# Spectral layers on one core: the last task's rows for the inverse W product loaded step by step into the first task's buffer, and held groups moved to other steps

## What is computed

```python
# layer 0
f = fft2(x, axes=(1, 2), norm='ortho'); Xh = (f.real - f.imag)[:, :, :46]
o1 = relu(einsum(Xk, w1[0]) + b1[0]); o2 = einsum(o1, w2[0]) + b2[0]
x = ifft2(softshrink(o2, 0.01), s=(H, W)).real + x
# layer 1
xf = rfft2(x, axes=(1, 2), norm='ortho')
o1r = relu(mm(xr, w1[0]) - mm(xi, w1[1]) + b1[0])
o1i = relu(mm(xi, w1[0]) + mm(xr, w1[1]) + b1[1])
o2r = softshrink(mm(o1r, w2[0]) - mm(o1i, w2[1]) + b2[0], 0.01)
o2i = softshrink(mm(o1i, w2[0]) + mm(o1r, w2[1]) + b2[1], 0.01)
y = irfft2(o2r + 1j * o2i, s=(H, W)) + x
```

## Time and profile before

| | |
|---|---|
| median of 3 runs | 519.47 us (517.39 to 521.99) |
| the profiled execution | 518.5 us |
| its span | 516.7 us |
| TensorE busy | 475.7 us, 92% |
| VectorE (DVE) / ScalarE (ACT) / GpSimd (POOL) busy | 59% / 41% / 34% |
| mean granted TensorE clock | 0.971 of full speed |
| DRAM read and written | 201 GB/s over the span |

### The profile page before, as it was taken

How to read it: one execution, slowest core, us unless ns; L and a number is a source line. 1 busy time by engine, 2 the same in 40 slices (tenths; PEclk the granted TensorE clock), 3 DMA queues, 4 the chain that set the end, 5 groups by cost and what they waited for, 6 DMA issues and landing times.

```text
span 516.7 us, 14864 instructions
## 1 busy us (share of the span) xinstructions
PE 475.7 (92%) x6144; PEld 341.0 (66%) x6144; DVE 306.7 (59%) x674; ACT 209.5 (41%) x473; POOL 173.1 (34%) x194
## 2 busy tenths in 40 slices
PE   3479999999999999999999999999999999998773
PEld 1157787767777677767777776767777777876531
DVE  6534455457754677457754677456764577567643
ACT  0025544643445443543354442554355433434201
POOL 9822313223341344223441244313442123222124
PEclk9859999999999999999999999999999999999967
DMA  8889763667989588977889688977989565644397
GB/s 182 264 229 258 198 192 91 148 204 193 261 230 238 158 229 245 231 207 186 256 238 219 173 198 256 234 201 182 261 222 256 158 176 158 145 100 129 114 257 226
DMA packets 76864, 104.63 MB, mean 203 GB/s; under 512 B 7777, under 2 KB 63319, under 8 KB 76798
## 3 DMA queue, kind: packets, MB, share of 16 engines
q1 hardware_dynamic: 57766, 56.74, 41.1%
q0 software_dynamic: 10608, 40.45, 29.5%
q10 hardware_dynamic: 8424, 6.49, 5.1%
HBM read 52.21 MB, written 51.43 MB: 201 GB/s over the span
## 4 chain that ended last, share of the span: by engine, by line
PE 79%; DVE 6%; DMA 6%; POOL 3%; ACT 2%; issue 2%; SPq 1%; ACTq 1%; POOLq 0%; DVEq 0%
PE ps L620 14%; PE ps L686 13%; PE ps L711 12%; PE ps L673 11%; PE ps L587 10%; PE ps L633 8%; PE ps L698 5%; PE ps L649 4%; PE ps L659 3%; DMA img<-x 2%; DVE img L566 2%; DVE ns L540 2%; POOL xs L384 2%; ACT p L457 1%; DVE nt L518 1%
## 5 line engine op out<-in xcount | busy, mean ns | idle before, releaser
L566 DVE TENSOR_TENSOR img<-ps,img 90x768 f32<-90x768 f32 x92 | 82.6, 900 | 20.3 <-PE ps L620 16.9
L384 POOL TENSOR_TENSOR xs<-xs,nt 128x360 f32<-128x360 f32 (+1 forms) x48 | 41.6, 866 | 147.9 <-DVE nt L518 120.6
L620 PE MATMUL ps<-jr,cst 64*90 64x384 f32 (+1 forms) x358 | 81.5, 525 | 6.7 <-DVE img L566 5.7
L587 PE MATMUL ps<-img,cst 128*64 128x384 f32 (+1 forms) x368 | 70.8, 500 | 9.7 <-DMA img<-x 9.7
L393 POOL DMA_DIRECT2D y<-img x42 | 34.8, 828 | 133.5 <-DVE img L566 133.2
L450 ACT ACTIVATE o<-ps,wt 97x180 f32<-97x180 f32 (+1 forms) x96 | 33.8, 406 | 107.6 <-PE ps L673 107.6
L633 PEld LDWEIGHTS ps<-cst,bt 128*64 128x64 f32 x1472 | 63.2, 141 | 20.4 <-issue 13.9
L540 DVE SCALAR_TENSOR_TENSOR ns<-p,ps 109x384 f32<-109x384 f32 x96 | 53.2, 554 | 37.8 <-ACT p L457 32.9
L633 PE MATMUL ps<-cst,bt 128*64 128x90 f32 x1472 | 69.0, 248 | 6.1 <-DMA bt<-scr_f 6.1
L686 PE MATMUL ps<-wt,o 128*64 128x96 f32 x1472 | 73.9, 249 | 0.2 <-DVE o L532 0.2
L686 PEld LDWEIGHTS ps<-wt,o 128*64 128x64 f32 x1472 | 64.9, 137 | 12.3 <-issue 12.3
(11 more groups left out here) (41 smaller groups left out, 403.0 us busy)
## 6 DMA issues: line engine op xcount, KB each, us to landing
y<-img POOLq DMA_DIRECT2D x35, 540.0 KB, 5.4
img<-x POOLq DMA_DIRECT2D x30, 540.0 KB, 8.3
scr_i<-et SPq DMA_DIRECT2D x48, 270.0 KB, 5.6
scr_f<-fs SPq DMA_DIRECT2D x154, 72.0 KB, 3.3
bt<-scr_f SPq DMA_DIRECT2D x40, 270.0 KB, 5.2
jr<-scr_i SPq DMA_DIRECT2D x48, 216.0 KB, 5.3
img<-x ACTq DMA_DIRECT2D x10, 540.0 KB, 6.9
y<-img SPq DMA_DIRECT2D x11, 270.0 KB, 3.5
```

The costliest lines, as they stand in the source:

```text
L384: nc.gpsimd.tensor_tensor(re, re, nt[s % 2][:, :, 0:kws(s), 0:H], ALU.subtract).then_inc(re_ok, 1)
L566: nc.vector.tensor_tensor(y, p, y, ALU.add).then_inc(i_add, 1)
L587: last = mm(ps[64 * r:64 * r + 64, P3 + g % 2, 0:(b - a) * HC], K["w_fwd"], img[t % IMGS][:, a:b, :].rearrange("p h c -> p (h c)"), start= ...
L620: last = mm(ps[0:W, B0 + r, 0:n], K["w_inv"][64 * r:64 * r + 64, :], set_rows(t, j)[64 * r:64 * r + 64, at, 0:n], start=True, stop=True)
```

## The change

- Held groups: loop steps 45, 46, 47 and 48 get 3, 3, 2 and 2 of them; groups 10 and 11 come behind the last inverse H product. `pair_of` gives these two the pairs P2 and P1.
- The last task's rows go into `f0`, all 12 groups. Behind the store of each step's inverse H product (from the second of task 7) SP waits for the store of the step before and loads that step's rows: 8 partitions of each half r for groups 0 to 10, and 8 for group 11, three transfers. The last step's rows are loaded at `last_rows`, half 0 and group 11 by SP, half 1 by ACT. The product of group 0 waits for all.
- The products of task 7 contract over 48 partitions (2 * KWP) instead of 64.
- LAST_POOL has three groups instead of four, with `p1` and one `et` buffer in turn. ACT issues the stores of these three, behind its last copy; SP the other nine.

```diff
--- before.py
+++ after.py
@@ -23,10 +23,11 @@
 STEPS = -(-KW // STEP)
 NSTEPS = TASKS * STEPS
 GROUPS = -(-H // 4)
+HELD = 10
 XCH = 8
 NXC = -(-H // XCH)
 IMGS, FS, BT, JR = 3, 4, 3, 3
-LAST_POOL = (1, 4, 7, 10)
+LAST_POOL = (1, 4, 7)
 JSETS = [(0, 3), (3, 6), (6, 9), (9, 11), (11, 12)]
 
 KH = [0] + [k for j in range(1, H // 2 + 1) for k in (j, H - j)]
@@ -115,7 +116,7 @@
         if i == 0 and t > 1:
             inv[s] = [("inv", t - 2, 9 + k) for k in range(3)]
     held = [("inv", TASKS - 2, g) for g in range(GROUPS)]
-    for s, n in ((NSTEPS - 2, 2), (NSTEPS - 1, 2), (NSTEPS, 3)):
+    for s, n in ((NSTEPS - 3, 3), (NSTEPS - 2, 3), (NSTEPS - 1, 2), (NSTEPS, 2)):
         inv[s], held = held[:n], held[n:]
     for s in range(NSTEPS + 2):
         t, i = divmod(s, STEPS)
@@ -147,7 +148,7 @@
             order.append(("t", s - 1))
         order += inv[s][2:3]
     order += held
-    order += [("rows", TASKS - 1, j) for j in range(len(JSETS))]
+    order.append(("last_rows",))
     order += [("inv", TASKS - 1, g) for g in range(GROUPS)]
     return order
 
@@ -218,7 +219,8 @@
         e_mm, e_act, e_dve = sem("e_product"), sem("e_copied_act"), sem("e_copied_dve")
         e_st = [sem(f"e{k}_stored") for k in range(2)]
         j_ld = [sem(f"j{k}_loaded") for k in range(JR)]
-        j_tail = [sem(f"last_set{j}_loaded") for j in range(JR, len(JSETS))]
+        l_ld = [sem(f"last_rows{k}_loaded") for k in range(2)]
+        y_last_act = sem("y_of_last_task_stored_act")
         i_mm, i_add = sem("inv_product"), sem("inv_added")
 
         order = schedule()
@@ -239,11 +241,22 @@
             n = t * len(JSETS) + j
             return sum(16 * set_dmas(m % len(JSETS)) for m in range(k, n + 1, JR))
 
-        def set_rows(t, j):
-
-            if t == TASKS - 1 and j >= JR:
-                return bt[j - JR][:, 0:(JSETS[j][1] - JSETS[j][0]) * 2 * HC].rearrange("p (g c) -> p g c", c=2 * HC)
-            return jr[bank_of(t, j)[0]]
+        def last_rows(i, r):
+
+            k0, k1 = 2 * STEP * i, min(2 * STEP * (i + 1), 2 * KWP)
+            rows = scr_i[TASKS - 1].rearrange("k e h c -> (k e) h c")[k0:k1]
+            four = rows[:, 0:H - 1, :].rearrange("q (g r s) c -> q g r (s c)", r=2, s=2)[:, :, r, :]
+            return four, f0[64 * r + k0:64 * r + k1, 0:GROUPS - 1, :], rows[:, H - 1, :], f0[k0:k1, GROUPS - 1, 0:HC]
+
+        def held_no(t, g):
+
+            return g - HELD if t == TASKS - 2 else -1
+
+        def pair_of(t, g):
+
+            if t == TASKS - 1:
+                return (P0, P1, P2, P3)[g % 4]
+            return (P2, P1, P3)[held_no(t, g) % 3] if held_no(t, g) >= 0 else P3
 
         def f_dmas(g):
             return 1 if g == GROUPS - 1 else 2
@@ -317,33 +330,41 @@
                     sp.wait_ge(e_dve, s + 1)
                     sp.dma_start(scr_i[t][STEP * i:STEP * i + STEP].rearrange("k e h c -> (e h) k c"),
                                  et[s % 2][0:2 * H, :, :]).then_inc(e_st[s % 2], 16)
+                    if t == TASKS - 1 and i > 0:
+                        sp.wait_ge(e_st[(s - 1) % 2], 16 * ((s - 1) // 2 + 1))
+                        for r in range(2):
+                            four, to, one, to_one = last_rows(i - 1, r)
+                            sp.dma_start(to, four).then_inc(l_ld[0], 16)
+                        sp.dma_start(to_one, one).then_inc(l_ld[0], 16)
                 if kind == "rows" or (kind == "inv" and what[0] < TASKS - 1 and what[1] in (2, 5)):
                     t, j = what if kind == "rows" else (what[0], jset[what[1]] + JR)
                     k, used = bank_of(t, j)
-                    landed = j_tail[j - JR] if t == TASKS - 1 and j >= JR else j_ld[k]
                     if j == 0:
                         for e in range(2):
                             sp.wait_ge(e_st[(t * STEPS + STEPS - 1 - e) % 2], 16 * ((t * STEPS + STEPS - 1 - e) // 2 + 1))
                     if not used:
                         sp.wait_ge(j_clr, j + 1)
-                    if t == TASKS - 1 and j >= JR:
-                        sp.wait_ge(a_mm, 2 * NT)
-                    elif used:
+                    else:
                         m = t * len(JSETS) + j - JR
                         sp.wait_ge(i_mm, m // len(JSETS) * GROUPS + JSETS[m % len(JSETS)][1])
                     g0, g1 = JSETS[j]
                     rows = scr_i[t].rearrange("k e h c -> (k e) h c")
                     if g0 == GROUPS - 1:
-                        sp.dma_start(set_rows(t, j)[0:2 * KWP, 0, 0:HC], rows[:, 4 * g0, :]).then_inc(landed, 16)
+                        sp.dma_start(jr[k][0:2 * KWP, 0, 0:HC], rows[:, 4 * g0, :]).then_inc(j_ld[k], 16)
                     else:
                         four = rows[:, 4 * g0:4 * g1, :].rearrange("q (g r s) c -> q g r (s c)", r=2, s=2)
                         for r in range(2):
-                            sp.dma_start(set_rows(t, j)[64 * r:64 * r + 2 * KWP, 0:g1 - g0, :], four[:, :, r, :]).then_inc(landed, 16)
-                if kind == "inv" and what[0] == TASKS - 1:
+                            sp.dma_start(jr[k][64 * r:64 * r + 2 * KWP, 0:g1 - g0, :], four[:, :, r, :]).then_inc(j_ld[k], 16)
+                if kind == "last_rows":
+                    sp.wait_ge(e_st[(NT - 1) % 2], 16 * ((NT - 1) // 2 + 1))
+                    four, to, one, to_one = last_rows(STEPS - 1, 0)
+                    sp.dma_start(to, four).then_inc(l_ld[0], 16)
+                    sp.dma_start(to_one, one).then_inc(l_ld[0], 16)
+                if kind == "inv" and what[0] == TASKS - 1 and what[1] not in LAST_POOL:
                     g, (h0, h1), (b, f) = what[1], hrows(what[1]), divmod(TASKS - 1, HALVES)
                     sp.wait_ge(*last_added(g))
                     sp.dma_start(out[b, h0:h1, :, f * HC:(f + 1) * HC].rearrange("h w c -> w h c"), img[(TASKS - 1) % IMGS][0:W, h0:h1, :]).then_inc(y_last, 16)
-            sp.wait_ge(y_last, 16 * GROUPS)
+            sp.wait_ge(y_last, 16 * (GROUPS - len(LAST_POOL)))
 
         @block.gpsimd
         def _(pool):
@@ -398,7 +419,8 @@
                     n, (h0, h1) = LAST_POOL.index(g), hrows(g)
                     pool.wait_ge(i_act, n + 1)
                     y = img[t % IMGS][0:W, h0:h1, :].rearrange("p (r s) c -> p r (s c)", r=2)
-                    nc.gpsimd.tensor_tensor(y, p1[0:W], y, ALU.add).then_inc(i_pool, 1)
+                    p = (p1[0:W], et[NT % 2][0:W].rearrange("p (r s) c -> p r (s c)", r=2))[n % 2]
+                    nc.gpsimd.tensor_tensor(y, p, y, ALU.add).then_inc(i_pool, 1)
                 if kind == "load" and what[0] % STEPS == 3 and what[0] // STEPS >= 2:
                     refill(what[0] // STEPS - 2, NXC - 1)
             for t in range(TASKS - IMGS, TASKS - 1):
@@ -461,14 +483,26 @@
                         act.wait_ge(e_st[s % 2], 16 * (s // 2))
                     act.wait_ge(e_mm, s + 1)
                     nc.scalar.activation(et[s % 2][0:2 * H, 0::2, :], ps[0:2 * H, P0, 0:2 * HC].rearrange("p (k c) -> p k c", c=HC), ACT.Copy).then_inc(e_act, 1)
+                if kind == "last_rows":
+                    act.wait_ge(e_st[(NT - 1) % 2], 16 * ((NT - 1) // 2 + 1))
+                    four, to, _, _ = last_rows(STEPS - 1, 1)
+                    act.dma_start(to, four).then_inc(l_ld[1], 16)
                 if kind == "inv" and what[0] == TASKS - 1 and what[1] in LAST_POOL:
                     t, g = what
-                    n, B0 = LAST_POOL.index(g), 2 * (g % 4)
+                    n, B0 = LAST_POOL.index(g), pair_of(t, g)
                     act.wait_ge(i_mm, t * GROUPS + g + 1)
                     act.wait_ge(d1_ss, 2 * NT)
-                    if n > 0:
-                        act.wait_ge(i_pool, n)
-                    nc.scalar.activation(p1[0:W], ps[0:W, B0:B0 + 2, 0:2 * HC], ACT.Copy).then_inc(i_act, 1)
+                    act.wait_ge(e_st[NT % 2], 16 * ((NT - 2) // 2 + 1))
+                    if n > 1:
+                        act.wait_ge(i_pool, n - 1)
+                    p = (p1[0:W], et[NT % 2][0:W].rearrange("p (r s) c -> p r (s c)", r=2))[n % 2]
+                    nc.scalar.activation(p, ps[0:W, B0:B0 + 2, 0:2 * HC], ACT.Copy).then_inc(i_act, 1)
+            b, f = divmod(TASKS - 1, HALVES)
+            for n, g in enumerate(LAST_POOL):
+                h0, h1 = hrows(g)
+                act.wait_ge(i_pool, n + 1)
+                act.dma_start(out[b, h0:h1, :, f * HC:(f + 1) * HC].rearrange("h w c -> w h c"), img[(TASKS - 1) % IMGS][0:W, h0:h1, :]).then_inc(y_last_act, 16)
+            act.wait_ge(y_last_act, 16 * len(LAST_POOL))
 
         @block.vector
         def _(dve):
@@ -556,7 +590,7 @@
                 if kind == "inv" and (what[0] < TASKS - 1 or what[1] not in LAST_POOL):
                     t, g = what
                     h0, h1 = hrows(g)
-                    B0 = P3 if t < TASKS - 1 else 2 * (g % 4)
+                    B0 = pair_of(t, g)
                     dve.wait_ge(i_mm, t * GROUPS + g + 1)
```

(44 more changed lines are left out.)

## The result

Over 17 runs each, the changed kernel takes 522.92 us (median) and the kernel before 519.42; the ratio of the two is 1.0068, with an interval of 1.0051 to 1.0086. The forecast was 0.8 us less than before, 518.7, with a range up to 521.8; measured were some 3.5 us more.

What follows compares the result with a forecast made beforehand. TensorE bound the steady steps; serial ACT/POOL pairs and output stores limited the tail. Removing 9.4 us of held groups returned 2.3 + 2.6 + 4.0; with an 18.6 us tail, 0.8 less: 518.7 us, range 515.0 to 521.8.

Steps and rivals of the forecast that it cites:

- (a): Loop steps 45 to 48: ten held groups instead of seven ahead of the last H product make it 2.3 us later.
- (b): Behind the loop: groups 10 and 11 no longer wait for an add, 0.7 + 0.4 us replacing 9.4 us of held groups.
- (c): Between loop and tail: row loads behind the last store land in 4.0 us; task 7's first product at 497.3, before 497.8.
- The last load: Two 8-partition row loads behind the last store: 2.8 us plus 1.2 us for POOL's store, 4.0 us to landing.
- The 1.2 us added for POOL's store: DMA time of POOL's 337 KB store of groups 10 and 11, issued shortly before the last row loads.
- the narrow load: Rival: 8-partition row load late before task 7's first product; at 7.5 us landing, 2.7 us slower, 522.2; chance 0.17.
- T0: Start of task 7's first inverse product, where the tail begins: forecast 497.3, against 497.8 before.
- The two pages' rules: At the last row loads: 8 of 16 engines, about 27 GB/s per port; load 6.1 instead of 4.0 us.
- The last store: Store of the last H product's copy, ahead of the last row loads: 2.6 us to land.
- (d): Task 7's products: 48 rows take the same 0.65 us a group; full clock regained 6.0 us after the tail starts.
- The rival of unpaired products: Task 7's products of 48 rows don't run side by side: 1.3 and 2.56 us a group, 522.1; chance 0.05.
- (e): Tail from task 7's first product to the end: 18.6 us instead of 18.9, DMA drain last instead of the POOL chain.

Runs made afterwards that it cites:

- the first experiment: The changed kernel with held groups back in their old places (2, 2 and 3 in loop steps 46 to 48), against the kernel before: 519.97 us, ratio 1.0020.
- the third: The changed kernel with held groups back in their old places and each step's rows loaded half a step earlier, against the kernel before: 519.59 us, ratio 1.0023.

## Why the prediction was wrong

*(a) Held groups moved into the loop: right.* Step 45 gained 1.84 us (forecast 1.88), step 46 0.48 (0.5), step 48 nothing (-0.1); the last store is issued 2.4 us later from c1, forecast 2.3. The first experiment gave 2.5 us back in the time, and its steps took 7.38 and 8.76 us as before.

*(b) Groups 10 and 11 behind the loop: right in mechanism.* They run back to back, and TensorE then has nothing to do, from 496.1 to 506.5, 10.4 us where the forecast had 6.

*(c) The rows: the step that failed.* Two terms were too small.

- The last load: 4.0 us forecast, 6.9 measured. The base, 2.8 us from two 144 KB loads into 48 partitions, was a price for a wide load. With the same bytes wide it would have been right (3.9). The 1.2 us added for POOL's store can't be checked closely: 0.6 was measured, beside a narrow load. The sum left out 2.9 us for the width, though the forecast named the narrow load as a rival; it said that no row could weigh it and then took the end that suited the wide rows. The 0.17 for this rival was too low. Its number from the slowest row, T0 = 500.8 (47.0 from c1), came within 0.7 us of the measured 47.7, and its 522.2 us for the whole within 0.7 of 522.9; the range ended below it, at 521.8. The two pages' rules of the Trainium skill, 6.1 us for the load and T0 = 499.4, were nearer than the forecast but 2.1 us short in T0 (45.6 from c1).
- The last store: 2.6 us forecast, 3.8 measured. The forecast looked at the load of step 46 only for what it holds up on SP, where it holds up nothing. But it is issued right behind the last store and moves its data beside it. A moved transfer has to be priced on the DMA engines too, not only on its queue.

Together 2.9 + 1.2 = 4.1 us, and T0 came 4.2 us later than forecast.

*(d) The products: right.* Four instructions of 48 rows take as long as those of 64, and the clock was regained 6.2 us after T0 (6.0 forecast). The rival of unpaired products is out: groups of four take 1.28 us at the lower clock, as before.

*(e) The tail: right in sum.* 18.7 us against 18.6 forecast and 18.9 before. The DMA slices are at nine tenths without a gap from 516.0 to 522.3, so the drain is last, not POOL (512.5 to 525.2 us in 40 slices, busy share in tenths):

```profile
DMA  7895689413899999999999999999999888761000
```

ACT's stores came from T0 + 8.5 on instead of 9.9: the first was issued at 515.00, where the last copy begins.

The forecast saw that the five held groups were the cover of the row load, and it priced what replaces them at nearly nothing net. The sign turned on a transfer that nothing covers any more, and for such a one the pessimistic bound decides.

## What to carry over

When work that covers a transfer is moved away, the transfer becomes the path, and its price must come from a row of the same shape. If none exists, take the slow bound: here it would have given the sign and nearly the size. Splitting a load into slices of few partitions was free while it was hidden (the steps kept their length in the first experiment); the last slice isn't, even if it has a sixth of the bytes, and the slice issued just ahead of the last store makes that store slower too.

## What the runs showed of the hardware

- A load of 264 KB in two halves of 8 partitions took 6.8 us from issue to landing, 288 KB in 48 partitions 3.9, and 528 KB in two halves of 16 partitions 6.7. Of 28 more loads of 8 partitions, none took under 6.1.
- With a load of 8 partitions on its way, the last 270 KB store landed in 3.7 to 4.0 us instead of 2.6, in four kernels of four. No run has a wide load in that place.
- A load of 8 partitions counts 8 packets of 4 bytes beside its data, one of 16 or 48 partitions 16.
- The clock falls and comes back at moments that differ from run to run: after T0 the lower clock (0.50) lasted 6.2 us in the changed kernel, 4.0 in the first experiment and 7.0 in the third. The third has its T0 1.0 us sooner than the first, from c1, and ended 0.9 us later.
